# Causal attention with scores and exponentials three tiles ahead of the results

## What is computed

```
y   = layernorm(x)
q   = (y @ Wq + bq) / sqrt(512)
k   = y @ Wk + bk
v   = y @ Wv + bv
scores  = where(causal, q @ k.T, -inf)      # 64 x 64 for each of the 16 batches, one head
weights = softmax(scores)
x = x + (weights @ v) @ Wo + bo
```

## Time and profile before

| | us |
|---|---|
| Median of 3 runs | 3143.86 |
| Lowest and highest run | 3139.40, 3143.93 |
| The profiled execution | 3139.76 |
| Its span, first to last instruction | 3138.0 |
| The causal attention stage in it, first score matmul to first matmul of `pj1` | 493.01 to 533.74 |

### The profile page before, as it was taken

One profiled execution on the slowest core, in us unless ns is written; L12 is line 12 of the kernel. 1 busy time (PEld: TensorE's weight loads), 2 busy tenths in 40 slices (PEclk: granted clock), 3 DMA queues, 4 the chain that ended last, 5 costly groups with the idle time before them and its releaser, 6 DMA issues. The chain is left out here.

```text
span 3138.0 us, 55451 instructions
## 1 busy us (share of the span) xinstructions
PE 2882.3 (92%) x23526; PEld 2273.9 (72%) x23532; DVE 1642.5 (52%) x3408; ACT 1168.0 (37%) x1834; POOL 85.2 (3%) x67
## 2 busy tenths in 40 slices
PE   6998997999989999999999999999999987889655
PEld 3443876788877888888888888888888775668522
DVE  4333524544454555555555555555555465764586
ACT  2212221333333444344443444433444332523384
POOL 0001001000000000000000000000000013010000
PEclk9999998999999999999999999999999988889877
DMA  7886010111211111101111011110111029411300
GB/s 269 317 286 242 1 44 24 41 41 60 80 51 49 46 46 38 41 14 46 46 38 41 15 46 46 38 40 17 44 46 38 25 72 148 63 35 47 119 1 27
DMA packets 169953, 213.86 MB, mean 68 GB/s; under 512 B 55920, under 2 KB 109168, under 8 KB 168832
## 3 DMA queue, kind: packets, MB, share of 16 engines
q1 hardware_dynamic: 148640, 206.40, 21.0%
q10 hardware_dynamic: 21088, 4.20, 1.1%
HBM read 197.97 MB, written 10.49 MB: 66 GB/s over the span
## 5 line engine op out<-in xcount | busy, mean ns | idle before, releaser
L91 PE MATMUL xa_J<-xa_c_hi,xa_wk_hi 128*128 128x402 f32 x1024 | 365.0, 356 | 4.9 <-ACT xa_kT L1944 3.6
L2056 DVE CUSTOM_DVE_ANT_0 xa_pr<-xa_S,xa_m 128x402 f32<-128x402 f32 x512 | 271.0, 572 | 166.0 <-PE xa_S L2205 166.0
L92 PE MATMUL xa_J<-xa_c_lo,xa_wk_hi 128*128 128x402 f32 x1024 | 354.7, 346 | 0.0
L93 PE MATMUL xa_J<-xa_c_hi,xa_wk_lo 128*128 128x402 f32 x1024 | 354.7, 346 | 0.0
L91 PE MATMUL xa_J<-xa_wv_hi,xa_c_hi 128*128 128x512 f32 (+1 forms) x832 | 335.4, 403 | 0.0
L93 PE MATMUL xa_J<-xa_wv_hi,xa_c_lo 128*128 128x512 f32 (+1 forms) x832 | 327.3, 393 | 0.0
L92 PE MATMUL xa_J<-xa_wv_lo,xa_c_hi 128*128 128x512 f32 (+1 forms) x832 | 327.3, 393 | 0.0
L1944 ACT ACTIVATE xa_kT<-xa_J,cl_bk 128x402 f32<-128x402 f32 x256 | 151.7, 593 | 458.9 <-PE xa_J L93 458.9
L2083 DVE TENSOR_TENSOR cl_v<-xa_J,cl_bv 128x512 f32<-128x512 f32 (+1 forms) x208 | 143.5, 690 | 263.4 <-PE xa_J L93 225.7
L1960 ACT ACTIVATE xa_pr<-xa_pr,xa_nm 128x1608 f32<-128x1608 f32 x128 | 208.6, 1632 | 95.0 <-DVE xa_nm L2072 95.0
L91 PEld LDWEIGHTS xa_J<-xa_c_hi,xa_wk_hi 128*128 128x128 f32 x1024 | 193.2, 189 | 66.9 <-ACT xa_kT L1944 43.5
(11 more groups left out here) (470 smaller groups left out, 5391.7 us busy)
## 6 DMA issues: line engine op xcount, KB each, us to landing
bl_rows<-in_ctx SPq DMA_DIRECT2D x40, 1024.0 KB, 8.8
main_x<-in_ctx_cols SPq DMA_DIRECT2D x192, 201.0 KB, 2.7
bl_cols<-in_ctx_cols SPq DMA_DIRECT2D x24, 1024.0 KB, 10.6
main_x<-in_ctx_cols SPq DMA_DIRECT2D x64, 197.5 KB, 3.2
moe_raw<-in_L_ffn_routed_w SPq DMA_DIRECT2D x24, 512.0 KB, 3.9
main_qoT<-in_L_attn_W SPq DMA_DIRECT2D x16, 512.0 KB, 3.6
bl_early<-in_ctx SPq DMA_DIRECT2D x8, 768.0 KB, 12.9
ternx_raw<-in_L_ffn_w SPq DMA_DIRECT2D x4, 1024.0 KB, 7.1
```

What stands on the lines that cost most here:

```text
L91: pe.matmul(out, w_hi, x_hi, start=first, stop=False)
L92: pe.matmul(out, w_hi, x_lo, start=False, stop=False)
L93: return pe.matmul(out, w_lo, x_hi, start=False, stop=last)
L2056: nc.vector.tensor_tensor_reduce(out=pr[:, r, ks], in0=S[:, r, 0:KG], in1=m[:, ks], scale=1.0, scalar=NEVER, op0=ALU.add, op1=ALU.max, acc ...
```

## The change

`S` gets three banks and `C` three, so that with the two of `T` all eight PSUM banks are in use. `sc`, `pr` and `pT` get four buffers each. The three lists are written in another order, by the same operations in the same number: three tiles of scores, masks, maxima and exponentials stand at the start; in step t of the loop the scores, mask, maximum and exponential are those of tile t + 3, the reciprocal, scaling and transpose those of tile t, the copy of `T`, the result and `split_hi` those of tile t - 1, and `split_lo` that of tile t - 2. The waits follow the new counts of buffers. In lines of the changed kernel, `scores` is L1260, `turn` L1268, `result` L1275, `front` L1297 and L1299, `normalise` L1303 and L1305, `copy_turned` L1311 and `exp` L1337.

```diff
--- before.py
+++ after.py
@@ -1218,20 +1218,24 @@
 def causal_attention_stage(nc, qT, kT, v, ident, c_hi, c_lo, prefetch):
 
 
+
     NEVER = -1e30
+    AHEAD, RING = 3, 4
     with ExitStack() as ctx:
         s = Space(nc, ctx, "ca")
         causal = s.sb("causal", [P, P])
-        sc = s.sb("sc", [P, 2, P])
-        pr = s.sb("pr", [P, 2, P])
-        pT = s.sb("pT", [P, 2, P])
+        sc, pr, pT = (s.sb(n, [P, RING, P]) for n in ("sc", "pr", "pT"))
         nm, rs, ri = s.sb("nm", [P, TILES]), s.sb("rs", [P, TILES]), s.sb("ri", [P, TILES])
-        S = s.ps("S", [P, 2, 512])
+        S = s.ps("S", [P, AHEAD, 512])
         T = s.ps("T", [P, 2, 512])
-        C = s.ps("C", [P, 2, 512])
+        C = s.ps("C", [P, 3, 512])
         (mask_steps, scored, masked, max_ready, exp_done, inv_ready, scaled, turned, pT_ready, summed, hi_ready,
          lo_ready) = (s.sem(n) for n in ("mask_steps", "scored", "masked", "max_ready", "exp_done", "inv_ready", "scaled",
                                          "turned", "pT_ready", "summed", "hi_ready", "lo_ready"))
+
+        def rows_of_tile(t):
+            return C[:, t % 3, :].rearrange("p (k c) -> p k c", c=P)
+
         with nc.Block() as block:
 
             @block.sync
@@ -1250,29 +1254,37 @@
             @block.tensor
             def _(pe):
                 def scores(t):
-                    if t >= 2:
-                        pe.wait_ge(masked, t - 1)
+                    if t >= AHEAD:
+                        pe.wait_ge(masked, t - AHEAD + 1)
                     for k in range(KC):
-                        last = pe.matmul(S[:, t % 2, 0:P], qT[:, k, t * P:(t + 1) * P], kT[:, k, t * P:(t + 1) * P],
+                        last = pe.matmul(S[:, t % AHEAD, 0:P], qT[:, k, t * P:(t + 1) * P], kT[:, k, t * P:(t + 1) * P],
                                          start=(k == 0), stop=(k == KC - 1))
                     last.then_inc(scored, 1)
 
-                scores(0)
-                for t in range(TILES):
-                    if t + 1 < TILES:
-                        scores(t + 1)
+                def turn(t):
                     pe.wait_ge(scaled, t + 1)
                     if t >= 2:
                         pe.wait_ge(pT_ready, t - 1)
-                    pe.transpose(T[:, t % 2, 0:P], pr[:, t % 2, :], ident[:]).then_inc(turned, 1)
+                    pe.transpose(T[:, t % 2, 0:P], pr[:, t % RING, :], ident[:]).then_inc(turned, 1)
+
+                def result(t):
                     pe.wait_ge(pT_ready, t + 1)
-                    if t >= 2:
-                        pe.wait_ge(hi_ready, t - 1)
-                        pe.wait_ge(lo_ready, t - 1)
+                    if t >= 3:
+                        pe.wait_ge(lo_ready, t - 2)
                     for m in range(KC):
-                        last = pe.matmul(C[:, t % 2, m * P:(m + 1) * P], v[:, t, m * P:(m + 1) * P], pT[:, t % 2, :],
+                        last = pe.matmul(C[:, t % 3, m * P:(m + 1) * P], v[:, t, m * P:(m + 1) * P], pT[:, t % RING, :],
                                          start=True, stop=True)
                     last.then_inc(summed, 1)
+
+                for t in range(AHEAD):
+                    scores(t)
+                for t in range(TILES):
+                    turn(t)
+                    if t + AHEAD < TILES:
+                        scores(t + AHEAD)
+                    if t:
+                        result(t - 1)
+                result(TILES - 1)
 
             @block.vector
             def _(dve):
@@ -1280,46 +1292,63 @@
 
                 def front(t):
                     dve.wait_ge(scored, t + 1)
-                    if t >= 2:
-                        dve.wait_ge(exp_done, t - 1)
-                    nc.vector.tensor_tensor(sc[:, t % 2, :], S[:, t % 2, 0:P], causal[:], ALU.add).then_inc(masked, 1)
+                    if t >= RING:
+                        dve.wait_ge(exp_done, t - RING + 1)
+                    nc.vector.tensor_tensor(sc[:, t % RING, :], S[:, t % AHEAD, 0:P], causal[:], ALU.add).then_inc(masked, 1)
                     dve.wait_ge(masked, t + 1)
-                    nc.vector.tensor_reduce(nm[:, t:t + 1], sc[:, t % 2, :], AX.X, ALU.max, negate=True).then_inc(max_ready, 1)
-
-                def back(t):
+                    nc.vector.tensor_reduce(nm[:, t:t + 1], sc[:, t % RING, :], AX.X, ALU.max, negate=True).then_inc(max_ready, 1)
+
+                def normalise(t):
                     dve.wait_ge(exp_done, t + 1)
                     nc.vector.reciprocal(ri[:, t:t + 1], rs[:, t:t + 1]).then_inc(inv_ready, 1)
                     dve.wait_ge(inv_ready, t + 1)
-                    nc.vector.tensor_scalar(pr[:, t % 2, :], pr[:, t % 2, :], ri[:, t:t + 1], None, ALU.mult).then_inc(scaled, 1)
+                    nc.vector.tensor_scalar(pr[:, t % RING, :], pr[:, t % RING, :], ri[:, t:t + 1], None, ALU.mult).then_inc(scaled, 1)
+
+                def copy_turned(t):
                     dve.wait_ge(turned, t + 1)
+                    if t >= RING:
+                        dve.wait_ge(summed, t - RING + 1)
+                    nc.vector.tensor_copy(pT[:, t % RING, :], T[:, t % 2, 0:P]).then_inc(pT_ready, 1)
+
+                def low(t):
+                    dve.wait_ge(hi_ready, t + 1)
+                    split_lo(nc, tile_of(c_lo, t), rows_of_tile(t), tile_of(c_hi, t)).then_inc(lo_ready, 1)
+
+                for t in range(AHEAD):
+                    front(t)
+                for t in range(TILES):
+                    normalise(t)
+                    if t + AHEAD < TILES:
+                        front(t + AHEAD)
+                    if t:
+                        copy_turned(t - 1)
                     if t >= 2:
-                        dve.wait_ge(summed, t - 1)
-                    nc.vector.tensor_copy(pT[:, t % 2, :], T[:, t % 2, 0:P]).then_inc(pT_ready, 1)
-                    dve.wait_ge(hi_ready, t + 1)
-                    split_lo(nc, tile_of(c_lo, t), C[:, t % 2, :].rearrange("p (k c) -> p k c", c=P),
-                             tile_of(c_hi, t)).then_inc(lo_ready, 1)
-
-                front(0)
-                for t in range(TILES):
-                    if t + 1 < TILES:
-                        front(t + 1)
-                    back(t)
+                        low(t - 2)
+                copy_turned(TILES - 1)
+                low(TILES - 2)
+                low(TILES - 1)
 
             @block.scalar
             def _(act):
-                def front(t):
+                def exp(t):
                     act.wait_ge(max_ready, t + 1)
-                    if t >= 2:
-                        act.wait_ge(turned, t - 1)
-                    nc.scalar.activation(pr[:, t % 2, :], sc[:, t % 2, :], ACT.Exp, bias=nm[:, t:t + 1],
+                    if t >= RING:
+                        act.wait_ge(turned, t - RING + 1)
+                    nc.scalar.activation(pr[:, t % RING, :], sc[:, t % RING, :], ACT.Exp, bias=nm[:, t:t + 1],
                                          accum_out=rs[:, t:t + 1]).then_inc(exp_done, 1)
 
-                front(0)
+                def high(t):
+                    act.wait_ge(summed, t + 1)
+                    split_hi(nc, tile_of(c_hi, t), rows_of_tile(t)).then_inc(hi_ready, 1)
+
+                for t in range(AHEAD):
+                    exp(t)
                 for t in range(TILES):
-                    if t + 1 < TILES:
-                        front(t + 1)
-                    act.wait_ge(summed, t + 1)
-                    split_hi(nc, tile_of(c_hi, t), C[:, t % 2, :].rearrange("p (k c) -> p k c", c=P)).then_inc(hi_ready, 1)
+                    if t + AHEAD < TILES:
+                        exp(t + AHEAD)
+                    if t:
+                        high(t - 1)
+                high(TILES - 1)
 
 
 EXPERTS, SHARED, HID = 8, 2, 256
```

## The result

| | median us | lowest to highest | runs |
|---|---|---|---|
| before | 3143.09 | 3139.40 to 3144.11 | 6 |
| changed | 3129.64 | 3129.05 to 3135.85 | 6 |

The ratio is 0.9962, with a 95% interval of 0.9950 to 0.9975: the changed kernel is 13.45 us faster by the medians, and by the interval between 8 and 16. The forecast was 3130 and 13.0 less.

A forecast was written before the change was run, and what follows sets the result against it. Causal attention was taken as bound by a chain round the engines once per tile, no engine being full. 13.9 us less at full clock, minus 0.9 for a half-clock spell, gave 13.0 less: 3130 us, range 3124 to 3138.

The forecast's parts named there:

- The start: Start of the causal attention stage: three tiles' scores and maxima ahead delay the first transpose, costing 0.86 us.
- Transpose and scores together: TensorE, from a transpose's start to the end of the scores behind it: 1.32 us, bounds 1.21 and 1.39.
- The step: Loop at full clock: 3.20 us per tile instead of 4.20, through scaling, transpose, scores, mask.
- The end and the sum: Last five results, after scores are over: last low part ends at 519.54, not 533.43; 13.9 us less at full clock.
- The clock: TensorE's clock in the stage: full except one short half-clock spell beginning in the loose 496 to 501.6, costing 0.9 us.
- Rivals 1 and 2: Stage at half clock: from near 506, 8.4 us less, chance 0.12; from the first looser steps, 1.4 us less, chance 0.07.
- The projection gives nothing back: Projection behind the stage: a full-clock start brings TensorE to its wait 1.4 us earlier, where it waits 2.3.
- Rival 4: Stage's loop: costlier hand-overs or copies behind the wrong low part, 0.5 us per tile, leave 9 less; chance 0.10.
- Rival 3: Stage and projection: TensorE stays at 1.2 GHz through both, 18 us slower; chance 0.03.
- The median: Whole kernel: the median of before, 3143.9, less 13.0 gives 3130.9, stated as 3130 us.

The follow-up runs named there:

- the loop with results in place: Changed kernel with copy, result, high part and low part of a tile back right behind its transpose: causal block 39.9 us, ratio 1.0007 to before.
- scores first only: Changed kernel with TensorE issuing the scores of tile t+3 ahead of the transpose of tile t: causal block 23.8 us, ratio 0.9953 to before.
- copy first only: Changed kernel with VectorE copying the transpose of t-1 ahead of the mask of t+3: causal block 25.7 us, ratio 0.9957 to before.
- before with the wait filled: Kernel before plus four useless fp32 matmuls per tile in TensorE's wait ahead of the transpose: causal block 35.5 us, ratio 0.9977 to before.
- both swaps with two banks: Changed kernel with scores ahead of transpose, copy ahead of mask, two tiles ahead, two banks and buffers: causal block 19.6 us, ratio 0.9930 to before.

## Why the prediction was right

**The start: 0.86 us later.** The first transpose came 3.12 us after the first scores' start before and 4.01 now, 0.89 later.

**Transpose and scores together: 1.32, bounds 1.21 and 1.39.** The transpose at 510.22 and the end of the scores behind it at 511.44 are 1.22 apart. The value taken was 0.10 too long, and the measured one lies at the lower bound: scores start 0.16 behind the transpose, with no further 0.11. That 0.11 lies between the result and the next transpose instead (509.22 to 510.22 is 1.00), where the working had 0.89.

**The step: 3.20.** Measured 3.12, which is 1.22 and 1.90. From the scores' end to the next transpose the working had 1.78 by way of TensorE and 1.88 by way of VectorE. Measured, TensorE's way is 0.90 + 1.00 = 1.90 and the scaling ends at 510.16, 0.06 ahead of the transpose: the two are level, and no wait for the scaling is left to see. Result 0.89 after the scores' end: from 508.32 to 509.22, 0.90. VectorE's wait for scores was to be 1.4 and is 1.32.

**The end and the sum.** From the first scores to the end of the last low part (494.59 to 520.78) the stage takes 26.19 us; the working at full clock gave 519.54 - 493.01 = 26.53. It took 40.41 before, so the gain was 14.2 at full clock against 13.9.

**The clock: full but for one short spell, worth 0.9.** This term was a guess between bounds, not worked out from a cause: the first profile had no spell, the second had one, which made the block 1.5 longer, and 0.9 lies between. Where such a spell came, it was in the loose start that the prediction named. What does not hold is the reason given, how busy TensorE had been: the loop with results in place was busy for the same 57% as before, for longer, and kept its clock. Rivals 1 and 2 did not come true: from the second result on the changed kernel held 2.4 GHz to the end of its results in both profiles. The Trainium skill says that where matmul groups cycle through PSUM banks with brief idle times, the clock goes back and forth (TensorE: Matmul & The Clock Gate, A second HAM failure mode: psum-queue depth-cycling). The trace of before agrees, with waits of 1.43 us and four changes of the clock; of the two profiles of the new order, with waits of 0.90, one agrees, with one fall near its start, and the other shows no change until its results were over.

**The projection gives nothing back.** It took 30.5 us before and 30.3 after, both with a start at half clock. The full-clock start was not in the changed kernel's first profile, but came in its second and in others: TensorE then waited 1.95 to 2.35 us ahead of its fifth unit, where 2.3 was worked out. What had not been worked out is below.

**Rival 4, later hand-overs,** is excluded by the 0.90 and by the steps. **Rival 3** did not happen.

**The median.** 3129.64 against 3130. That they agree so closely is in part luck. The sum was 3143.9 less 13.0, 3130.9; with more runs the median of before is 3143.09, 0.8 lower, and the gain was 0.45 larger, and both errors go the same way. The stated 3130 had been rounded down by 0.9, which hides most of them, and the interval of the gain, 8 to 16 us, is far wider than any of these.

## What to carry to other kernels

On engines that work in order, how far ahead the first stage of a chain runs was worth little here; what counted is which waits stand in front of which work on each engine. Write down for one step the chain from each wait to the next, and put ahead of a wait every operation whose inputs are ready: that took this stage from 40.8 to 26.6 us, and two further swaps to 19.6 with the memory it had at the start.
A loop that leaves TensorE waiting (1.81 of 4.20 us here) can also pay in clock, as it did before, so a shortened chain can give more than its own sum: 5.3 us more here.

## What the runs showed of the hardware

A start at full clock did not help the projection, and could hurt it. In the execution with only TensorE's swap it began at 2.4 GHz, reached its fifth unit early, waited there, and fell to 1.2 GHz more than 8 us later (the second stretch). TensorE in order of time, and the stretches:

```profile
519.24 0.47 PE L91 MATMUL pj_out<-attn_w_hi,attn_a_hi 128*128 128x512 f32 x1 [1.68 <-PEq L1239]
...
532.74 0.50 PE L91 MATMUL pj_out<-attn_w_hi,attn_a_hi 128*128 128x512 f32 x1 [2.35 <-DVE main_x L1162]
```

```profile
519.00:541.00 22.00, 17.58 (x76) 13.77 (x76) 17.20 (x29) 5.37 (x9) 11.78 (x8) 1.00 0.06 13
541.00:545.00 4.00, 3.97 (x13) 3.25 (x14) 2.33 (x4) 2.35 (x4) 0.00 (x0) 0.57 0.00 0
545.00:551.00 6.00, 4.69 (x25) 3.60 (x23) 3.81 (x6) 1.09 (x2) 0.00 (x0) 1.00 0.00 0
```

The projection took 32.2 us there instead of 30.3. Seven profiles have full clock over its first 12 us. In three (scores first only, copy first only, before with the wait filled) the clock fell as here and it took 31.9 to 32.2; in three it fell right behind the wait of 2 us and in one not at all, and it took 30.2 to 30.5. Its shortest, 29.1 us, is in the first profile of both swaps with two banks, where it began at half clock. Which of its waits lets the clock fall was not tested.

The same code also differed by up to 3 us in the experts' block from one execution to the next, and the granted clock over that block was 1.00 in the one of 351.1 us and 0.99 in the one of 353.9. Whether the clock is all of that difference stays open.
